# Softmax attention with scores computed transposed on four row tiles

## The reference

```python
q = _qdq(x) @ _qdq(wq).T + bq
k, v = jnp.split(cond @ wkv.T + bkv, 2, axis=-1)
# heads: q (B, N, H, Dh), k and v (B, M, H, Dh); N = 56, M = 1500, Dh = 16
attn = jax.nn.softmax(jnp.einsum('bnhd,bmhd->bhnm', q, k) * scale, axis=-1)
o = jnp.einsum('bhnm,bmhd->bnhd', attn, v).reshape(B, N, C)
out = _qdq(o) @ _qdq(wp).T + bp
```

## Time and profile before

| | |
|---|---|
| median of 3 runs | 2786.24 us (2786.07 to 2787.38) |
| the profiled execution | 2787.42 us, span 2785.7 us |
| mean granted TensorE clock | 0.976 of full speed |
| busy over the span | TensorE 2635.4 us, VectorE 1902.0, ScalarE 1501.6, GpSimd 1430.6 |
| softmax stage, its steady part | 1170 to 2460 us from the span's start |
| feed-forward | from 2491 us |

### The profile page before, as it was taken

One profiled execution on the slowest core, in us unless ns is written; L12 is line 12 of the kernel. 1 busy time (PEld: TensorE's weight loads), 2 busy tenths in 40 slices (PEclk: granted clock), 3 DMA queues, 4 the chain that ended last, 5 costly groups with the idle time before them and its releaser, 6 DMA issues. The chain is left out here.

```text
span 2785.7 us, 62598 instructions
## 1 busy us (share of the span) xinstructions
PE 2635.4 (95%) x23470; PEld 2232.7 (80%) x23470; DVE 1902.0 (68%) x3171; ACT 1501.6 (54%) x2575; POOL 1430.6 (51%) x1355
## 2 busy tenths in 40 slices
PE   5999999999898997699999999999999999989998
PEld 3999999999765664488888888888888888868998
DVE  4888888888744667466666666666666666655654
ACT  2666666666323443365666566565565565543443
POOL 2888888888535886244344344334334434422222
PEclk9999999999989998799999999999999999999999
DMA  4554444454282444110111111011011011023000
GB/s 121 166 155 143 143 154 143 144 154 143 74 242 88 131 131 129 48 47 26 47 46 36 36 47 46 25 47 46 25 47 46 25 47 46 25 75 108 8 7 14
DMA packets 110941, 225.29 MB, mean 81 GB/s; under 512 B 32800, under 2 KB 81040, under 8 KB 106864
## 3 DMA queue, kind: packets, MB, share of 16 engines
q1 hardware_dynamic: 78912, 196.98, 23.1%
q10 hardware_dynamic: 28736, 19.01, 2.3%
q0 software_dynamic: 3216, 8.29, 0.9%
HBM read 193.24 MB, written 27.33 MB: 79 GB/s over the span
## 5 line engine op out<-in xcount | busy, mean ns | idle before, releaser
L1632 DVE TENSOR_SCALAR_CACHE_REDUCE a_prob<-a_s 112x1500 f32<-112x1500 f32 x256 | 440.0, 1719 | 117.8 <-PE a_s L1732 117.3
L1744 PEld LDWEIGHTS a_p<-ident,a_prob 112*125 112x125 f32 x3072 | 380.6, 188 | 112.2 <-issue 103.3
L1592 ACT COPY a_probT<-a_p 125x448 f32<-125x448 f32 x512 | 248.5, 533 | 392.7 <-PE a_p L1744 392.7
L1744 PE MATMUL a_p<-ident,a_prob 112*125 112x112 f32 x3072 | 445.7, 281 | 2.2 <-ACT a_prob L1585 1.4
L1585 ACT ACTIVATE a_prob<-a_prob,a_mxs 112x1500 f32<-112x1500 f32 x256 | 396.4, 1548 | 64.6 <-DVE a_prob L1632 64.6
L443 POOL TENSOR_TENSOR l_rows_lo<-l_raw,l_rows_hi 125x512 fp32r<-125x512 f32 x192 | 273.0, 1422 | 105.7 <-ACT l_rows_hi L478 105.7
L446 POOL TENSOR_TENSOR l_phik_lo<-l_phif,l_phik_hi 125x512 fp32r<-125x512 f32 x192 | 297.3, 1549 | 11.8 <-ACT l_phik_hi L484 11.8
L542 DVE TENSOR_TENSOR l_ctxT_lo<-l_rawT,l_ctxT_hi 128x500 fp32r<-128x500 f32 x192 | 213.7, 1114 | 95.5 <-ACT l_ctxT_hi L461 95.5
L1510 POOL TENSOR_TENSOR a_free<-a_one 128x1 f32<-128x1 f32 x96 | 18.5, 193 | 496.1 <-PE a_a L80 488.7
L80 PE MATMUL l_k<-T_Wk_lo,l_ctxT_hi 128*125 128x256 f32 x768 | 225.0, 293 | 36.0 <-DVE l_phif L559 26.3
L80 PE MATMUL a_a<-T_wv_lo,a_ctxT_hi 128*125 128x256 f32 x768 | 231.8, 302 | 0.0
(11 more groups left out here) (313 smaller groups left out, 7073.5 us busy)
## 6 DMA issues: line engine op xcount, KB each, us to landing
l_rawT<-in_ctxT SPq DMA_DIRECT2D x32, 1500.0 KB, 6.3
a_rawT<-in_ctxT SPq DMA_DIRECT2D x32, 1500.0 KB, 6.2
l_raw<-in_ctx SPq DMA_DIRECT2D x32, 1344.0 KB
e_wall<-in_L_ffn_w_gate_up SPq DMA_DIRECT2D x8, 1024.0 KB, 14.1
W_hi<-e_xn ACTq DMA_DIRECT2D x32, 192.0 KB, 2.3
W_lo<-e_xn ACTq DMA_DIRECT2D x32, 192.0 KB, 3.0
l_raw<-in_ctx SPq DMA_DIRECT2D x32, 156.0 KB
e_xb<-sorted_x SPq DMA_DIRECT2D x35, 129.0 KB, 2.1
```

The source lines that it names most:

```text
L1592: act.copy(p_target(j, f), p_source(i)).then_inc(p_read[i], 1)
L1632: dve.tensor_scalar(prob[j % 2][:, :].rearrange("p (g n) -> p g n", g=KG), s_bank[0:TT, :, 0:GW], 1.0, None, ALU.mult, ALU.min, accum_out= ...
L1744: mm = pe.transpose(p_bank[i][0:CH, q * TT:(q + 1) * TT], prob[j % 2][:, ch * CH:(ch + 1) * CH], K["ident"][0:TT, 0:TT])
```

## The change

The scores are computed transposed: positions on the partitions, queries in the columns. The stationary operand is a chunk of 125 keys of one pair of heads (32 rows), and the moving one is that pair's masked queries (112 columns). Four pairs lie on four row tiles and write to four banks, and `S` is now one of three groups of 500 positions of a half `k` of the heads, 16 matmuls. They are full fp32 instead of three split products; `keyT` and `qbd` have no low parts any more, and the turned keys and queries are gone. Probabilities come out as `X` needs them, so all `P` go.

The maximum now lies across partitions. ScalarE copies each group of scores into a ring of eight buffers (`C`), VectorE takes elementwise maxima of groups (`P`, `J`), then over chunks (`M`). TensorE transposes the result (`T`), VectorE reduces it to one value per query and head (`R`), TensorE spreads it over the partitions again (`M`). ScalarE keeps a copy (`Z`). VectorE subtracts it from the first group (`U`), GpSimd from the other two (`U`, called late shifts below). ScalarE takes exponentials (`E`) in the ring.

Values have a column of ones beside the 16 of each head, so `X` gives sums as well. `X` does the heads of a pair apart (`r`), 56 columns each, 96 matmuls for a half. ScalarE copies the result (`O`), a product with `sumsel` spreads the sums (`F`), and VectorE divides (`D`) into `attT` and a second tile `odd`. The bias of the values is added when they are copied. The loop's body holds four batches.

```diff
-    "S0 P70' P71' K10 P72' K11 "
...
+    "F0' V1 V3 S10 V2 K12 T0 S11 +K00 M0 "
+    "X1' S12 V5 +K01 V4 F1' +S00 +V0 +K10 +S01 "
+    "T1 +K02 M1 X0 +S02 +K11 "
 ).split()
 SCALAR_ORDER = (
...
+    "K11 E10' E11' C10 E12' C11 K12 Z0 +K00 O1' "
+    "C12 E00 +K01 E01 +C00 E02 +C01 Z1 +K02 +K10 "
+    "O0 +C02 "
 ).split()
 VECTOR_ORDER = (
...
+    "P0 U1' J0 V1 V3 M0 V2 D0' R0 P1 "
+    "U0 V5 J1 V4 D1' M1 +V0 R1 "
 ).split()
 GPSIMD_ORDER = (
-    "L1' Q1 "
-    "+C0 +C1 L0 +C2 +Q0 "
+    "C1 U01' U02' C2 Q1 U11' U12' +Q0 +C0 "
 ).split()
...
-            def turn_queries(b):
...
             def spread(b, k):
...
+                pool.tensor_tensor(qbd[:, k, :, :], mask2[:, :, :], mine.unsqueeze(1).to_broadcast([P, 2, L]), ALU.mult).then_inc(q_made[k], 1)
+
+            def shift_late(b, u, k, g):
+
+                n = KC * b + k
+                pool.wait_ge(tops_kept, n + 1)
+                now = scores_of(u, k, g)
+                pool.tensor_tensor(now, now, tops[:, :, :].unsqueeze(2).to_broadcast([CH, 4, 4, TT]), ALU.subtract).then_inc(shifted_late, 1)
...
+            def score_copy(b, u, k, g):
+
+                n = KC * b + k
+                act.wait_ge(s_full, HALF * n + g + 1)
...
+                act.copy(chunks_flat(scores_of(u, k, g)), s_bank[0:CH, :, 0:TG]).then_inc(s_copied, 1)
...
+            def pair(b, u, k):
+
+                n = KC * b + k
+                dve.wait_ge(s_copied, HALF * n + 2)
+                dve.tensor_tensor(chunks_flat(top[:, :, :, :]), s_bank[0:CH, :, 0:TG], chunks_flat(scores_of(u, k, 0)), ALU.max).then_inc(paired, 1)
+
+            def join(b, k):
...
+                dve.tensor_tensor(flat, s_bank[0:CH, :, 0:TG], flat, ALU.max).then_inc(joined, 1)
+
+            def maximum(b, k):
...
+                dve.tensor_reduce(most[:, :, :], top[:, :, :, :].rearrange("p j c n -> p j n c"), AX.X, ALU.max).then_inc(most_done, 1)
...
             def outputs(b, k):
...
+                dve.reciprocal(inv[:, :], x_bank[:, sums_at]).then_inc(inv_done, 1)
+                dve.wait_ge(inv_done, n + 1)
+                for r, to in enumerate((K["attT"], K["odd"])):
+                    at = slice(r * L, (r + 1) * L)
+                    dve.tensor_tensor(to[:, k, bass.ds(b * L, L)], outs[:, at], inv[:, at], ALU.mult).then_inc(out_done, 1)
...
+            def scores(b, k, g):
+                n = KC * b + k
+                if g == 0:
                     pe.wait_ge(q_made[k], b + 1)
+                    wait(pe, joined, n)
+                else:
+                    pe.wait_ge(s_copied, HALF * n + g)
+                    if g == 2:
+                        pe.wait_ge(paired, n + 1)
+                wait_pieces(b, [f"K{k}{g}"])
+                for q in range(4):
+                    at = g * GW + q * CH
+                    for j in range(4):
+                        rows = slice(j * PW, (j + 1) * PW)
+                        mm = pe.matmul(s_bank[0:CH, j, q * TT:(q + 1) * TT], keyT[rows, k, at:at + CH],
+                                       qbd[rows, k, :, :].rearrange("p r n -> p (r n)"), start=True, stop=True)
                 mm.then_inc(s_full, 1)
...
+                pe.wait_ge(exp_done, HALF * (n + 1))
+                wait(pe, out_done, 2 * n)
...
+                for r in range(2):
+                    for ch in range(NC):
+                        for j in range(4):
+                            mm = pe.matmul(x_bank[j * PW:j * PW + HV, r * L:(r + 1) * L], val[u % 2][:, ch, 8 * k + 2 * j + r, :],
+                                           scores_of(u, k, ch // 4)[:, j, ch % 4, r * L:(r + 1) * L], start=(ch == 0), stop=(ch == NC - 1))
+                mm.then_inc(x_full, 1)
...
+                        for r, src in enumerate((K["attT"], K["odd"])):
+                            q = 2 * k + r
+                            mm = pe.transpose(s_bank[t % 2][0:TT, q * P:(q + 1) * P], src[:, k, at:at + TT], K["ident"][:, :])
```

More of the change, by code:

```diff
@@ L1486, in batch @@
                 load(b + 1)
-                for k in range(KC):
-                    sp.wait_ge(q_made[k], b + 1)
-                turn_queries(b + 1)
-            turn_queries(0)
-            load(0)
-            with sp.Fori(0, B - 1) as b:
-                batch(b)
         @block.gpsimd
@@ L1555, in batch @@
+            def batch(b, u):
+                for w, of, at in turns(GPSIMD_ORDER, b, u):
                     if w[0] == "C":
@@ new lines, in keep, with batch @@
+            def keep(b, k):
+                n = KC * b + k
+                act.wait_ge(x_full, n + 1)
+                wait(act, out_done, 2 * n)
+                act.copy(outs[:, :], x_bank[:, 0:TT]).then_inc(x_kept, 1)
+            def batch(b, u):
+                for w, of, at in turns(SCALAR_ORDER, b, u):
+                    if w[0] == "C":
+                        score_copy(of, at, int(w[1]), int(w[2]))
+                    elif w[0] == "E":
+                        exp(of, at, int(w[1]), int(w[2]))
+                    elif w[0] == "Z":
+                        keep_tops(of, int(w[1]))
+                    elif w[0] == "K":
+                        key_copy(of, w)
+                    elif w[0] == "O":
+                        keep(of, int(w[1]))
@@ L1613, in _ @@
+            for b in (-1, 0, 1):
+                batch(b, b % TURN)
+            with act.Fori(0, (B - 4) // TURN) as i:
+                for m in range(TURN):
+                    batch(TURN * i + 2 + m, (2 + m) % TURN)
+            for b in (B - 2, B - 1, B):
+                batch(b, b % TURN)
         @block.vector
         def _(dve):
-            def key_low(b, w):
-                i = PIECE_BANK[w]
-                dve.wait_ge(k_hi, k_count(w, b))
-                dve.scalar_tensor_tensor(out=keys(w).lo, in0=a_bank[i][:, 0:GW], scalar=key_bias(w), in1=keys(w).hi.bitcast(F32),
-                                         op0=ALU.add, op1=ALU.subtract).then_inc(a_read[i], 1)
@@ L1662, in batch @@
+            def batch(b, u):
+                for w, of, at in turns(VECTOR_ORDER, b, u):
+                    if w[0] == "V":
+                        value_copy(of, at, w)
+                    elif w[0] == "P":
+                        pair(of, at, int(w[1]))
+                    elif w[0] == "J":
+                        join(of, int(w[1]))
+                    elif w[0] == "M":
                         maximum(of, int(w[1]))
-                    elif w[0] == "P":
-                        p_copy(of, int(w[1]), int(w[2]))
@@ L1687, in _ @@
+            with dve.Fori(0, (B - 4) // TURN) as i:
+                for m in range(TURN):
+                    batch(TURN * i + 2 + m, (2 + m) % TURN)
+            for b in (B - 2, B - 1, B):
+                batch(b, b % TURN)
         @block.tensor
         def _(pe):
-            pe.wait_ge(masks_set, 2)
+            pe.wait_ge(ones_set, 3)
+            pe.wait_ge(x_cleared, 1)
             def wait_pieces(b, pieces):
@@ L1773, in batch, with sums @@
+                mm.then_inc(x_full, 1)
+            def sums(b, k):
+                pe.wait_ge(x_kept, KC * b + k + 1)
+                pe.matmul(x_bank[:, sums_at], K["sumsel"][:, :], outs[:, :], start=True, stop=True).then_inc(sums_full, 1)
+            def batch(b, u):
+                for w, of, at in turns(TENSOR_ORDER, b, u):
+                    if w[0] == "S":
+                        scores(of, int(w[1]), int(w[2]))
                     elif w[0] in "KV":
                         piece(of, w)
-            batch(-1)
@@ L1785, in feed_forward @@
+            for b in (-1, 0, 1):
+                batch(b, b % TURN)
+            with pe.Fori(0, (B - 4) // TURN) as i:
+                for m in range(TURN):
+                    batch(TURN * i + 2 + m, (2 + m) % TURN)
+            for b in (B - 2, B - 1, B):
+                batch(b, b % TURN)
 def feed_forward(nc, a, out, K):
@@ L1821, in feed_forward @@
         of = lambda t, g: t[:, QG * g:QG * (g + 1)]
+        half_of = lambda part: range(2 * part, 2 * part + 2)
         MW = MC // WP
@@ L2100, in down @@
                 mm.then_inc(d_full, 1)
[L2102 removed]
+            rows(0, 0)
+            rows(0, 1)
             turned(0)
```

514 lines of the change are left out of this document (207 added, 307 removed).

## The result

| | before | after |
|---|---|---|
| median | 2786.43 us (4 runs, 2786.07 to 2787.38) | 2719.55 us (4 runs, 2718.26 to 2722.02) |
| ratio | | 0.9761, 95% interval 0.9744 to 0.9777 |
| span of the profiled execution | 2785.7 us | 2717.7 us |
| mean granted clock over the span | 0.976 | 0.954 |

What follows compares the result with a forecast made beforehand. TensorE was taken to bound the softmax stage: 33.3 us a batch against 41.25 gains 246.5 over 31 batches, ends add 7, so 2787.4 becomes 2547.9, predicted as 2547 us; range 2492 to 2640, some 80%.

Steps and rivals of the forecast that it cites:

- The sum: TensorE's work per softmax batch: scores, values, key and value pieces, transposes, foldings, 31.3 us; 32.4 with changes of kind.
- 0.9 of waits: TensorE waiting behind ScalarE copies and VectorE maxima: 0.9 us a batch, making 33.3 instead of 41.25.
- the second rival: Waits grow: output products with two SBUF operands blocked by GpSimd's long operations; 35.2 us a batch, 2607 us, chance 23%.
- Row tiles load in parallel: Score calls: loads into different row tiles overlap, a pass costs 0.111 us, a call 1.08, 6.5 a batch.
- the slower rival: Score row tiles load one after another: 3.74 us a call, 48.3 a batch, 3013 us, chance 6%.
- Rounds of `X` shrink: Value products: half the streaming makes a round 0.054 us, 48 rounds 2.6, so 5.2 a batch.
- the rival with 9.7 us: Value product rounds can't get shorter than 0.101 us: TensorE has 36.9 a batch, 2659 us, chance 8%.
- The ends: Work outside the steady batches: last batch's tail, feed-forward's additions and earlier first scores, together +7 us.
- the first scores: Start of the score stage: some 2 us sooner, with one key piece instead of three.
- the last batch's tail: From the last batch's first scores to the feed-forward's first transposes: 52 us instead of 48, so +4.

Runs made afterwards that it cites:

- the flat version: The changed kernel with TensorE's loop written out, no jump back: 2688.95 us, 0.9666 of the kernel before.
- the combined version: The changed kernel with TensorE's loop written out, output products reading PSUM, and value products split in runs of 96: 2605.17 us, 0.934 of the kernel before.
- the two maxima: Strided reduction replaced by elementwise maxima of 896 and 448 columns: 2698.84 us in the changed kernel, 2526.2 in the combined version.
- the body of four: The kernel before with only TensorE's loop body made four batches long, same instructions and order: 2830.64 us, ratio 1.0152.
- the two best runs: The combined version with most of each later context load left out, 2536.42 us, and the combined version with the two maxima, 2526.2 us.

## Why the prediction was wrong

**The sum has no term for the supply of instructions.** That is the step that failed. It counted TensorE's matmuls per batch and forecast 32.4 us, plus 0.9 of waits, all of them for copies and maxima of other engines. Of the waits in the profile after, 80.6 us per 1000 are issue, some 3.1 us in each batch of 38.7, and none was in the sum. (38.7: the scores start from 1156.1 to 2385.8, by the order 31 batches and about three quarters.) The description of the change says that the loop's body now holds four batches, and shows value products that are twice as many and half as long; neither got a price or a rival. The runs give three parts of it, whose prices overlap: the jump (31 us by the flat version), runs of 192 passes (44 us by splitting them, 25 in the combined version), packets late behind the context load (17 us in this kernel, 69 in the combined version, where it was the only one left).

**Two prices of VectorE.** The reduction was taken at 2.02 us as an operation over 1792 columns; reading at a stride it is 3.4 (21 us net by the two maxima). The output's products were in the sum at 0.27 each, although the text quotes 739 ns in the median and names the mechanism as the second rival: 1.3 us for the first of each half, 50 us by moving an operand to PSUM. That rival had the mechanism right; its 2607 knew neither the reduction's length nor the issue stops. Together the reduction and the products made TensorE wait 42.3 us per 1000 for `maximum`, 1.6 a batch, where 0.9 was allowed for all waits.

**The clock.** The sum takes every price at a granted 1.00. After, it was 0.96: behind the stop of 3.02 us the value pieces' matmuls start 0.21 us apart (1709.29, 1709.50) at a granted 0.50, and in the next piece 0.12 again (1712.36, 1712.48). Busy time per batch was 38.7 x 1069.63/1230 = 33.7 us instead of 32.4, so 1.3 of the 5.4 us a batch that are missing; idle time is 5.0 instead of 0.9, the other 4.1. Over 31 batches that is 167 of the 172 us; the ends have the other 5. That the clock falls behind a stop is seen at each jump of the body of four; that it falls because of it was not tested by itself. In all versions where the stops vanished it stood at 1.00.

**What was right.** Row tiles load in parallel (1.07 us a call, not 3.74), so the slower rival fell. Rounds of `X` shrink: 145 passes in 2.0 us, 13.8 ns each, which makes 2.65 for the 192 of a half (2.6 forecast), so the rival with 9.7 us fell too, and with it the floor of some 25 ns between starts that the Trainium skill (TensorE: Matmul & The Clock Gate, "Wait — 56ns, not 53.3ns?") states; on four column tiles these rows contradict it. ScalarE's and GpSimd's prices were right to 0.1 us. The ends came to about +12 for +7: the feed-forward took +6.9 for +5, and of the first scores, 8.4 us earlier for 2, and the last batch's tail, some 13 longer for 4, the errors partly cancel, which is luck. Right, too, was the sum for TensorE: without the load, the combined version has its scores from 1161.4 to 2204.4, which by the same count of batches is 32.9 us each, for 32.4 and small waits. The 2536 and 2526 of the two best runs lie 11 and 21 us below the 2547 that was expected, but with edits that the forecast kernel does not have. TensorE's work was forecast rightly; what keeps it from doing that work was not.

**What stays open.** Why the two maxima freed the combined version of its stops. They slowed GpSimd (its smallest operation, L1459, went from 197 to 617 ns, which I put to VectorE) and so moved the split after which the load is issued. By the packet records the load starts 0.5 to 0.8 us after the start of a run of value products in the combined version, and 2.1 to 2.7 us with the two maxima; but it meets as many matmuls per us in both (26). That the later start frees TensorE is argued, not shown. Also open is why only a run of 192 passes stalls without a load. A rough estimate from the combined version points at the supply: 134 packets for 17031 matmuls are 127 matmuls a packet, so a run of 192 uses one and a half packets in 2.65 us, and no two packets start closer than 3.25 us there. No run tests this.

## What to carry to other kernels

When a change replaces few long instructions by many short ones, or makes a loop's body longer, count the instructions too: look for packets of the instruction queue and for idle time with "issue" in front of it, and price a jump back. Such a stall is as much a matter of what else uses the DMA engines at that moment: try the big load away before restructuring the compute. An elementwise VectorE operation on two SBUF operands beside a busy GpSimd wants one of them in PSUM, and one with a stride must be priced from a strided row.

## What the runs showed of the hardware

- A loop of TensorE whose body held one batch (some 470 matmuls) had no stop for instructions; with two or four batches each jump back cost 7.0 to 7.3 us, about 4 of it idle and the rest in a stretch at a granted clock of 0.50. Straight code of the same instructions cost nothing.
- At every stop that the profile calls "issue", in the changed kernel and in the combined version, TensorE went on 1.2 to 1.6 us after an instruction packet had landed (up to 2.0 at a jump). Beside a 1.5 MB load such packets started late, and the combined version stopped for up to 2.6 us; with parts of 0.5 MB for at most 1.5, and without the load not at all but for one stop of 0.2.
- 145 fp32 passes of 56 columns on four column tiles took 2.0 us, 13.8 ns each, and 32 passes of 112 columns on four row tiles take 1.07 us.
- A VectorE operation over 1792 columns takes 2.0 us with adjacent elements and 3.4 to 3.55 with a stride of 448 bytes (read) or 16 (written).
- A product of 56 columns in VectorE took 216 to 2755 ns with two SBUF operands and GpSimd busy beside it, and 215 to 218 with one of them in PSUM.
- The best version here, flat, PSUM outputs, split runs and two maxima, takes 2526.2 us, 0.9066 of the kernel before.
